# Local attention: q's norm applied on GpSimd, and v projected in the next tile's step

## The chip, the cores and the metric

The kernel runs on one core of one Trainium2 chip. Its time is the device time of one execution in microseconds (us), and a kernel's figure is the median of its runs.

The core has five engines that matter here, each with its own instruction stream that is worked off in order: TensorE (PE in the profile; its weight loads are listed apart as PEld), VectorE (DVE), ScalarE (ACT), GpSimd (POOL) and SyncE (SP), which issues the DMAs. They meet through semaphores. Matmuls read SBUF and write PSUM; GpSimd reads and writes SBUF only.

## The reference

The program is a chain of four blocks over activations of 2048 tokens by 128 features, with a layer norm behind each: an attention, a mixture of experts, a second attention, and a transformer of two layers (`LAYERS = 2`), each with local attention and a gated MLP. The change lies in the local attention alone. Per layer, with 8 heads of 64 and windows of 64 tokens that look back one window:

```python
h = shift_token(x)
q, k, v = jnp.split(h @ wqkv, 3, axis=-1)      # each split into heads
q = l2norm(q) * qs
k = l2norm(k) * ksc
q, k = rotary_xpos(q, k)
o = local_attention(q, k, v)                   # softmax(8 q k^T + mask) v, key windows w-1 and w
x = x + o @ wo
```

`l2norm` divides each head's vector by its own length, one number for each token and head.

## The kernel before

The 2048 tokens are `NT` = 16 tiles of 128; four tiles (`TPB`) are a batch, and t = n % 4 is a tile's place in its batch. Each layer's local attention (`local_attention`) is a loop over the 16 tiles, software pipelined by hand: every engine has a function `step(n)` that works on the scores of tile n, finishes tile n-1 and prepares tiles n+1 and n+2. Tile 0 runs in `first` in layer 0 (it overlaps the end of the second attention), tile 15 in `last`, where the MLP begins. Nothing reorders instructions: an engine does them in the order of the code, and waits where a semaphore's count is not there yet. In the middle of a layer all inputs are in SBUF; DMAs play no part in these steps.

The order of `step(n)` on each engine:

- TensorE: `scores(n, 0)` (first two masks by an identity matmul, L2261, then the products, L2267), `values(n-1, 1)` (L2294, L2304), `project_qk(n+2)` (L2232), the transposes of the probabilities `turn_p(n, 0)` and `turn_p(n, 1)` (L2277), `scores(n, 1)`, `values(n, 0)`, `spread(n-1)` (L2315), `turn_qk(n+1, 0)`, which transposes q, `turn_p(n, 2)`, `turn_qk(n+1, 1)`, which transposes k (both L2251), `turn_p(n, 3)`, `output(n-1)` (L2322), `project_v(n+2)` (L2243). `scores(n+1, 0)` of the next step waits until k of tile n+1 has been copied out of PSUM.
- VectorE: `rowmax` of head pairs 0 and 1 (L2135 and L2140), `squares(n+1)` (sums and their clamp, L2126 and L2130), `copy_pT(n, 0)` (L2144), `rope_sum(n+1)` (L2122), `rowmax` of pairs 2 and 3, `normalise(n-1)` (L2155), `copy_pT(n, 2)`, `reciprocal(n)` (L2149), `rope_c(n+2)` (L2115), `add_y(n-1)` (L2159).
- ScalarE: the exponentials of pairs 0 and 1 (L2039), `copy_o(n-1)` (L2050), `copy_pT(n, 1)` (L2045), `copy_qk(n+2)` (L1997), the exponentials of pairs 2 and 3, `copy_qT(n+1)` (L2019), `copy_pT(n, 3)`, `copy_kT(n+1)` (L2026, L2028), the squares of tile n+2 (L2002), `copy_v(n+2)` (L2012 for three tiles in four, L2015 for all).
- GpSimd: `norms(n+1)` (the powers L1958 and L1967, k's product L1963), `widen(n)` (L1974), `rope_s(n+2)` (two instructions, L1950).

The norm is `rn = ssqc ** -0.5`, a power of 128 x 8 numbers on GpSimd, one instruction for q and one for k. Only k is multiplied by its norm (128 x 512 numbers, into `k_n`). q stays as it comes out of the rotary sum, and its norm enters later as the `scale` of the exponential; so the row maximum needs a second small VectorE instruction, L2140, which multiplies the maximum by `rn`.

`project_v` writes PSUM bank 7 (`m_ps`), which `spread`, `normalise`, `output` and `add_y` also use; it therefore waits for `add_y` of an earlier tile.

Of the kernel before, what the change touches and what calls it, by code (L numbers as in the profile page):

```python
# [15 lines left out]
P = 128  # L16
# [3 lines left out]
TPB = S // P  # L20
# [1795 lines left out]
def local_attention(nc, keep, tiles, layer):  # L1816
# [41 lines left out]
    sqr = sb("sqr", [P, 2 * INNER])  # L1858
    ssq = sb("ssq", [P, 2 * NH2])
    ssqc = sb("ssqc", [P, 2 * NH2])  # L1860
    rn = sb("rn", [P, TPB, 2 * NH2])
    neg_half = sb("neg_half", [P, 2 * NH2])
    qk_c = sb("qk_c", [P, 2, INNER])
    qk_s = sb("qk_s", [P, 2, INNER])
# [2 lines left out]
    qT = sb("qT", [P, 2, PAIRS, P])  # L1867
    kT = sb("kT", [P, 2, 2, 3, P])
    v = sb("v", [P, TPB, INNER])
    negraw = sb("negraw", [P, NH2])  # L1870
    negmax = sb("negmax", [P, NH2])
    den = sb("den", [P, 2, NH2])
    rden = sb("rden", [P, NH2])
# [60 lines left out]
    def gpsimd(pool):  # L1934
# [19 lines left out]

        def norms(n, t):

            pool.wait_ge(ssq_done, n + 1)
            nc.gpsimd.tensor_tensor(rn[:, t, NH2:2 * NH2], ssqc[:, NH2:2 * NH2], neg_half[:, 0:NH2], ALU.pow  # L1958
                                    ).then_inc(rn_step, 1)
            pool.wait_ge(rope_add, n + 1)  # L1960
            pool.wait_ge(rn_step, 2 * n + 1)
            wait_past(pool, qkT_mm, 2 * n)
            nc.gpsimd.tensor_tensor(k_n[:, :].rearrange("p (h d) -> p h d", d=HD2),  # L1963
                                    qk_r[:, 1, :].rearrange("p (h d) -> p h d", d=HD2),
                                    rn[:, t, NH2:2 * NH2, None].broadcast_to([P, NH2, HD2]), ALU.mult
                                    ).then_inc(qk_norm, 1)
            nc.gpsimd.tensor_tensor(rn[:, t, 0:NH2], ssqc[:, 0:NH2], neg_half[:, 0:NH2], ALU.pow  # L1967
                                    ).then_inc(rn_step, 1)
            pool.wait_ge(rn_step, 2 * n + 2)

        def widen(n):
            pool.wait_ge(recip, n + 1)
# [18 lines left out]
    def scalar(act):  # L1991
# [40 lines left out]
        def exps(n, t, k):  # L2032
            j = PAIRS * n + k
            act.wait_ge(max_done, j + 1)
            if k == 0:
                wait_past(act, recip, n - 1)
            for i in range(2):
                u = head(k, i)
                ins = nc.scalar.activation(prob[:, k % 2, keys(t, i)], ps[:, 2 + k % 2, keys(t, i)], ACT.Exp,  # L2039
                                           bias=negmax[:, u:u + 1], scale=rn[:, t, u:u + 1], accum_out=den[:, t % 2, u:u + 1])  # L2040
            ins.then_inc(exp_done, 1)

        def copy_pT(n, t, k):
# [8 lines left out]
        def step(n):  # L2052
            t = n % TPB
            exps(n, t, 0)
            exps(n, t, 1)
            if n:
                copy_o(n - 1)
            copy_pT(n, t, 1)
            if n + 2 < NT:
                copy_qk(n + 2)  # L2060
            exps(n, t, 2)
            exps(n, t, 3)
            if n + 1 < NT:
                copy_qT(n + 1, (t + 1) % TPB)
            copy_pT(n, t, 3)
            if n + 1 < NT:
                copy_kT(n + 1, (t + 1) % TPB)
            if n + 2 < NT:
                squares(n + 2)
            if n + 2 < NT:  # L2070
                copy_v(n + 2, (t + 2) % TPB)

        def last(mlp):

# [12 lines left out]
        def first(low_half):  # L2087

            exps(0, 0, 0)
            exps(0, 0, 1)  # L2090
            copy_pT(0, 0, 1)
            copy_qk(2)
            exps(0, 0, 2)
            exps(0, 0, 3)
            copy_qT(1, 1)
            low_half()
            copy_pT(0, 0, 3)
            copy_kT(1, 1)
            squares(2)
            copy_v(2, 2)  # L2100

        return LocalScalar(step, first, last, copy_qk, squares, copy_v, copy_qT, copy_kT)

    def vector(dve):
# [27 lines left out]
        def rowmax(n, t, k):  # L2132
            dve.wait_ge(s_mm, PAIRS * n + k + 1)
            us = slice(head(k, 0), head(k, 1) + 1, 2)
            nc.vector.tensor_reduce(negraw[:, us],  # L2135
                                    ps[:, 2 + k % 2, 0:2 * KEYS].rearrange("p (i c) -> p i c", i=2) if t
                                    else blocks(t, ps[:, 2 + k % 2, 0:2 * KEYS]), AX.X, ALU.max, negate=True).then_inc(raw_max, 1)
            dve.wait_ge(raw_max, PAIRS * n + k + 1)
            dve.wait_ge(rn_step, 2 * n + 2)
            nc.vector.tensor_tensor(negmax[:, us], negraw[:, us], rn[:, t, us], ALU.mult).then_inc(max_done, 1)  # L2140

        def copy_pT(n, t, k):
            dve.wait_ge(pT_mm, PAIRS * n + k + 1)
# [70 lines left out]
    def tensor(pe, ahead):  # L2214
# [158 lines left out]
        def first(turn_x):  # L2373
# [604 lines left out]
```

## Time and profile before

| | us |
|---|---|
| median of 3 runs | 1655.27 |
| lowest, highest | 1651.87, 1656.19 |
| the profiled execution, its own time | 1658.24 |
| its span in the profile | 1656.5 |
| scores of layer 0's tile 0 start | 1146.23 |
| scores of layer 0's tile 15 start | 1332.01 |
| scores of layer 1's tile 0 start | 1404.25 |
| scores of layer 1's tile 15 start | 1585.65 |

The last four lines are times from the span's start, where the first mask of a tile's scores starts. Over the span TensorE is busy 92%, VectorE 69%, ScalarE 65%, GpSimd 31%. The two stretches of the local attention are some 186 and 181 us of the span for 15 steps each.

A timeline row gives an instruction or a run of like ones: start, duration, engine, line, operation, output from inputs, how many, and in brackets the idle time of its engine before it and what ended it. Matmuls are pipelined, so what a group of them costs TensorE is the distance from its start to the next group's start, not its printed duration.

### The profile page before, as it was taken

The page shows a single profiled execution, that of the slowest core. Times are in us where ns is not written, and L with a number is a line of the kernel's source. Part 1 is how long each engine was busy: PE and PEld are TensorE (multiplying, and loading weights), DVE is VectorE, ACT ScalarE, POOL GpSimd, SP SyncE. Part 2 cuts the span into 40 slices and gives each one's busy share as a digit, 9 for nine tenths or more (in the row PEclk, how much of TensorE's full clock was granted, in tenths as well). Part 3 has the DMA queues.
Part 4 walks back from the last instruction along what each step waited for, and adds up shares of the span by engine and source line. Part 5 has one row for each costly group of instructions (what it writes and reads, how often), then busy time and mean ns, then how long its engine had stood idle before and what let it go on. Part 6 is the DMA issues. An engine that isn't in the chain of part 4 may idle for free. (4 is left out here: it accounts for less than half of the span.)

```text
span 1656.5 us, 30452 instructions
## 1 busy us (share of the span) xinstructions
PE 1525.9 (92%) x10190; PEld 1033.3 (62%) x10190; DVE 1137.0 (69%) x2336; ACT 1083.1 (65%) x2499; POOL 517.0 (31%) x476
## 2 busy tenths in 40 slices
PE   7999999999979999999979999996999888999986
PEld 6777777777667888888854333333566555566654
DVE  2666666666658777777787788864677654767755
ACT  2555555555567888888856577754777755777751
POOL 1222222222232112222110000015767633776732
PEclk9999999999979999999987799978999999999998
DMA  7000000000011221221100000000000000000000
GB/s 236 2 2 0 0 0 0 0 0 0 1 49 57 77 76 64 76 76 55 59 1 1 1 1 1 1 1 1 1 1 1 1 1 0 1 2 1 1 1 26
DMA packets 18993, 36.35 MB, mean 22 GB/s; under 512 B 5764, under 2 KB 11008, under 8 KB 16704
## 3 DMA queue, kind: packets, MB, share of 16 engines
q1 hardware_dynamic: 18896, 35.09, 6.4%
q8 instruction: 57, 0.93, 0.2%
q14 instruction: 40, 0.33, 0.1%
HBM read 33.91 MB, written 1.18 MB: 21 GB/s over the span
## 5 line engine op out<-in xcount | busy, mean ns | idle before, releaser
L915 DVE TENSOR_TENSOR m_hidp<-m_hid,m_hidp 128x512 fp32r<-128x512 f32 x256 | 181.6, 737 | 76.6 <-ACT m_hidp L831 75.4
L305 ACT ACTIVATE a_prob<-ps,a_negmax 128x512 f32<-128x512 f32 (+3 forms) x256 | 134.0, 526 | 146.7 <-DVE a_negmax L381 146.7
L836 ACT ACTIVATE m_hid<-ps,pre_w 128x512 f32<-128x512 f32 x256 | 175.7, 687 | 63.2 <-PE ps L1064 62.5
L1064 PE MATMUL ps<-c_sb_st,m_w1p 128*128 128x512 f32 x768 | 192.1, 399 | 0.0
L1119 PE MATMUL ps<-m_hidp,m_w2p 128*128 128x512 f32 x768 | 190.0, 396 | 0.2 <-DVE m_hidp L915 0.2
L1441 ACT ACTIVATE c_sb_pT<-ps 128x512 f32<-128x512 f32 x256 | 137.4, 601 | 79.6 <-PE ps L1654 78.6
L1511 DVE TENSOR_REDUCE c_sb_negmax<-ps 128x1 f32<-128x512 f32 x240 | 152.7, 684 | 47.2 <-PE ps L1639 47.1
L265 POOL TENSOR_TENSOR a_qk_r<-a_qk_c,a_qk_s 128x512 f32<-128x512 f32 x64 | 81.3, 1270 | 324.0 <-DVE a_qk_s L372 324.0
L2039 ACT ACTIVATE l_sb_prob<-ps,l_sb_negmax,l_sb_rn 128x192 f32<-128x192 f32 (+1 forms) x256 | 124.1, 494 | 69.5 <-DVE l_sb_negmax L2140 69.5
L1064 PEld LDWEIGHTS ps<-c_sb_st,m_w1p 128*128 128x128 f32 x768 | 145.5, 190 | 37.8 <-issue 3.0
L1119 PEld LDWEIGHTS ps<-m_hidp,m_w2p 128*128 128x128 f32 x768 | 144.1, 188 | 35.8 <-DVE m_hidp L915 0.4
L831 ACT ACTIVATE m_hidp<-m_hid 128x512 fp32r<-128x512 f32 x256 | 153.9, 630 | 0.0
L381 DVE TENSOR_REDUCE a_negmax<-ps 128x1 f32<-128x512 f32 (+3 forms) x256 | 112.9, 483 | 23.3 <-PE ps L478 23.3
L2135 DVE TENSOR_REDUCE l_sb_negraw<-ps 128x2 f32<-128x384 f32 (+1 forms) x128 | 66.3, 518 | 76.1 <-PE ps L2267 76.1
L386 DVE COPY a_probT<-ps 128x512 f32<-128x512 f32 (+3 forms) x128 | 61.0, 477 | 81.2 <-PE ps L488 81.2
L500 PEld LDWEIGHTS ps<-a_probT,a_lat 128*64 128x64 f32 x1280 | 68.2, 136 | 66.8 <-issue 61.5
L500 PE MATMUL ps<-a_probT,a_lat 128*64 128x128 f32 x1280 | 98.1, 282 | 10.2 <-issue 9.1
L478 PE MATMUL ps<-a_qkT 64*128 64x256 f32 (+3 forms) x512 | 104.6, 485 | 0.0
L488 PE MATMUL ps<-keep_ident,a_prob 128*128 128x128 f32 x640 | 96.1, 281 | 0.0
L1639 PE MATMUL ps<-c_sb_st 32*128 32x512 f32 x240 | 84.1, 532 | 10.4 <-ACT c_sb_pT L1441 10.4
L1950 POOL TENSOR_TENSOR c_sb_pT<-c_sb_pT,l_sb_tab_s 128x512 f32<-128x512 f32 x64 | 82.7, 1311 | 17.4 <-ACT c_sb_pT L1997 16.8
L759 POOL CAST m_w1p<-pre_w 128x512 fp32r<-128x512 f32 x16 | 10.3, 643 | 245.8 <-DMA pre_w<-w1T 180.6
(247 smaller groups left out, 3253.9 us busy)
## 6 DMA issues: line engine op xcount, KB each, us to landing
m_gate_all<-m_gates_d SPq DMA_DIRECT2D x16, 1024.0 KB, 4.7
pre_w<-w1T SPq DMA_DIRECT2D x14, 258.0 KB, 2.6
pre_w<-w2T SPq DMA_DIRECT2D x14, 256.0 KB, 2.7
pre_wqkv<-wqkv SPq DMA_DIRECT2D x2, 768.0 KB
keep_x<-x SPq DMA_DIRECT2D x1, 1024.0 KB, 10.0
out<-keep_x SPq DMA_DIRECT2D x4, 256.0 KB, 2.5
keep_xT<-xT SPq DMA_DIRECT2D x1, 768.0 KB, 5.2
pre_m_w<-l_w SPq DMA_DIRECT2D x2, 341.0 KB
```

Source lines behind the costliest of these rows:

```text
L305: nc.scalar.activation(prob[:, u % 4, 0:width(p)], score_ps(b, p, j)[:, 0:width(p)], ACT.Exp, bias=negmax[:, u:u + 1], accum_out=den[:, b ...
L381: nc.vector.tensor_reduce(negmax[:, u:u + 1], score_ps(b, p, j)[:, 0:width(p)], AX.X, ALU.max, negate=True).then_inc(max_done, 1)
L478: nc.tensor.matmul(score_ps(b, p, j)[:, 0:width(p)], qkT[r, b % 2, 0, i * P:(i + 1) * P], qkT[r, b % 2, 1, 0:width(p)], start=False, stop= ...
L500: ins = nc.tensor.matmul(o_ps[64 * j:64 * j + 64, i * P:(i + 1) * P], lat[:, b * TPB + t, :], probT[:, j, t * P:(t + 1) * P], start=(t == ...
L831: nc.scalar.activation(hidp[:, c % 2, 0, f, :], hid[:, c % 2, f, :], ACT.Copy).then_inc(high_done, 1)
L836: nc.scalar.activation(hid[:, c % 2, f, :], ps[:, f, :], ACT.Gelu, bias=w1[:, k, FF + f:FF + f + 1]).then_inc(gelu_done, 1)
L915: nc.vector.tensor_tensor(hidp[:, c % 2, 1, f, :], hid[:, c % 2, f, :], hidp[:, c % 2, 0, f, :], ALU.subtract).then_inc(low_done, 1)
L1064: ins = nc.tensor.matmul(ps[:, f, :], w1p[:, k, a, f * P:(f + 1) * P], xp[:, b, c, :], start=(i == 0), stop=(i == 2))
L1119: ins = nc.tensor.matmul(ps[:, 4 + c % 2, :], w2p[:, k, a, f, :], hidp[:, c % 2, b, f, :], start=(f == 0 and i == 0), stop=(f == FB - 1 an ...
L1441: nc.scalar.activation(pT[:, m % 2, g + i, t, :], ps[:, pair(exp_turn(e)).start + i, :], ACT.Exp, scale=SCALE).then_inc(exp_done, 1)
L1511: nc.vector.tensor_reduce(negmax[:, m % 2, t, g + i:g + i + 1], ps[:, pair(max_turn(k)).start + i, :], AX.X, ALU.max, negate=True).then_in ...
L2039: ins = nc.scalar.activation(prob[:, k % 2, keys(t, i)], ps[:, 2 + k % 2, keys(t, i)], ACT.Exp, bias=negmax[:, u:u + 1], scale=rn[:, t, u: ...
```

## The change

Two edits of `local_attention`, together.

First, q is multiplied by its norm on GpSimd, in place, before k. The order in `norms` becomes: power for q, wait for the rotary sum, product for q, power for k, product for k. Before it was: power for k, wait for the rotary sum, product for k, power for q. The transposes of q now wait for q's product. In return the row maximum is final as it comes out of PSUM: L2140, its semaphore and its wait for the norm go, and the exponential has no `scale` from a tile.

Second, v of tile n+1 is projected in step n behind `values(n-1, 1)` and ahead of `project_qk(n+2)`, where v of tile n+2 was projected at the end of step n. ScalarE copies it behind `copy_pT(n, 1)` and ahead of `copy_qk(n+2)`, where it did so at the end of the step. The waits inside `project_v` and `copy_v` are unchanged. No DMA and no SyncE instruction is touched.

```diff
         def norms(n, t):
             pool.wait_ge(ssq_done, n + 1)
-            nc.gpsimd.tensor_tensor(rn[:, t, NH2:2 * NH2], ssqc[:, NH2:2 * NH2], neg_half[:, 0:NH2], ALU.pow
-                                    ).then_inc(rn_step, 1)
-            pool.wait_ge(rope_add, n + 1)
-            pool.wait_ge(rn_step, 2 * n + 1)
-            wait_past(pool, qkT_mm, 2 * n)
-            nc.gpsimd.tensor_tensor(k_n[:, :].rearrange("p (h d) -> p h d", d=HD2),
-                                    qk_r[:, 1, :].rearrange("p (h d) -> p h d", d=HD2),
-                                    rn[:, t, NH2:2 * NH2, None].broadcast_to([P, NH2, HD2]), ALU.mult
-                                    ).then_inc(qk_norm, 1)
-            nc.gpsimd.tensor_tensor(rn[:, t, 0:NH2], ssqc[:, 0:NH2], neg_half[:, 0:NH2], ALU.pow
-                                    ).then_inc(rn_step, 1)
-            pool.wait_ge(rn_step, 2 * n + 2)
+            for w in range(2):
+                nc.gpsimd.tensor_tensor(rn[:, heads(w)], ssqc[:, heads(w)], neg_half[:, 0:NH2], ALU.pow
+                                        ).then_inc(rn_step, 1)
+                if w == 0:
+                    pool.wait_ge(rope_add, n + 1)
+                else:
+                    wait_past(pool, qkT_mm, 2 * n)
+                pool.wait_ge(rn_step, 2 * n + w + 1)
+                nc.gpsimd.tensor_tensor((k_n[:, :] if w else qk_r[:, 0, :]).rearrange("p (h d) -> p h d", d=HD2),
+                                        qk_r[:, w, :].rearrange("p (h d) -> p h d", d=HD2),
+                                        rn[:, heads(w), None].broadcast_to([P, NH2, HD2]), ALU.mult
+                                        ).then_inc(qk_norm, 1)
...
             for i in range(2):
                 u = head(k, i)
                 ins = nc.scalar.activation(prob[:, k % 2, keys(t, i)], ps[:, 2 + k % 2, keys(t, i)], ACT.Exp,
-                                           bias=negmax[:, u:u + 1], scale=rn[:, t, u:u + 1], accum_out=den[:, t % 2, u:u + 1])
+                                           bias=negmax[:, u:u + 1], accum_out=den[:, t % 2, u:u + 1])
...
             copy_pT(n, t, 1)
+            if 1 < n + 1 < NT:
+                copy_v(n + 1, (t + 1) % TPB)
             if n + 2 < NT:
                 copy_qk(n + 2)
...
-            if n + 2 < NT:
-                copy_v(n + 2, (t + 2) % TPB)
...
-            nc.vector.tensor_reduce(negraw[:, us],
+            nc.vector.tensor_reduce(negmax[:, us],
...
-                                    else blocks(t, ps[:, 2 + k % 2, 0:2 * KEYS]), AX.X, ALU.max, negate=True).then_inc(raw_max, 1)
-            dve.wait_ge(raw_max, PAIRS * n + k + 1)
-            dve.wait_ge(rn_step, 2 * n + 2)
-            nc.vector.tensor_tensor(negmax[:, us], negraw[:, us], rn[:, t, us], ALU.mult).then_inc(max_done, 1)
+                                    else blocks(t, ps[:, 2 + k % 2, 0:2 * KEYS]), AX.X, ALU.max, negate=True).then_inc(max_done, 1)
...
             pe.wait_ge(raw_done, min(n + 2, NT))
-            pe.wait_ge(qk_norm if w else rope_add, n + 1)
+            pe.wait_ge(qk_norm, 2 * n + w + 1)
...
                 values(n - 1, (t - 1) % TPB, 1)
+            if 1 < n + 1 < NT:
+                project_v(n + 1, (t + 1) % TPB)
             if n + 2 < NT:
                 project_qk(n + 2, (t + 2) % TPB)
...
                 output(n - 1)
-            if n + 2 < NT:
-                project_v(n + 2, (t + 2) % TPB)
```

`first` loses its `project_v(2, 2)` and `copy_v(2, 2)` in the same way.

## Rows read from the trace of the kernel before

**Rows 1.** Windows of layer 0's steps 4, 5, 6 and 14: busy of PE, PEld, DVE, ACT, POOL; clock; DMA
```profile
1198.90:1210.66 11.76, 10.16 (x80) 6.77 (x78) 8.43 (x17) 9.09 (x26) 8.56 (x7) 1.00 0.01 2
1210.66:1222.71 12.05, 11.44 (x83) 7.40 (x82) 8.66 (x17) 9.73 (x26) 8.68 (x7) 1.00 0.01 1
1222.71:1235.35 12.64, 11.81 (x91) 7.82 (x90) 8.77 (x17) 9.35 (x25) 8.58 (x7) 1.00 0.00 1
1320.91:1332.01 11.10, 9.40 (x85) 6.65 (x84) 7.47 (x16) 7.49 (x23) 7.18 (x6) 1.00 0.01 2
```

**Rows 2.** The chain that ended last, in step 6: start, duration, what
```profile
1229.70 0.65 DVE l_sb_negmax L2140
1230.37 1.10 ACT l_sb_prob L2039 x4
...
1233.98 0.30 DVE keep_x L2159
```

**Rows 3.** Timeline of TensorE in step 6
```profile
1222.71 0.49 PE L2261 MATMUL ps<-pre_wmask,pre_identb 128*128 128x384 bf16 x2
...
1226.97 0.82 PE L2277 MATMUL ps<-keep_ident,l_sb_prob 128*128 128x128 f32 x6
...
1230.07 0.66 PE L2315 MATMUL ps<-keep_ident,c_sb_pT 128*128 128x128 f32 x4
1230.56 0.60 PE L2251 MATMUL ps<-keep_ident,c_sb_pT 128*128 128x128 f32 x4
...
1231.90 0.60 PE L2251 MATMUL ps<-keep_ident,c_sb_pT 128*128 128x128 f32 x4
1232.51 0.55 PE L2277 MATMUL ps<-keep_ident,l_sb_prob 128*128 128x128 f32 x3
...
1234.42 1.10 PE L2243 MATMUL ps<-pre_wqkv,keep_xT 128*128 128x512 f32 x2 [0.48 <-DVE keep_x L2159]
```

**Rows 4.** Timeline of VectorE, ScalarE and GpSimd in step 6, and v's copy
```profile
1227.50 0.56 DVE L2144 COPY c_sb_pT<-ps 128x384 f32<-128x384 f32 x1 [0.67 <-PE ps L2277]
1227.98 1.22 DVE L2122 TENSOR_TENSOR c_sb_pT<-c_sb_pT 128x1024 f32<-128x1024 f32 x1
1228.22 1.02 ACT L1997 ACTIVATE c_sb_pT<-ps 128x1024 f32<-128x1024 f32 x1
1229.27 1.04 POOL L1963 TENSOR_TENSOR c_sb_pT<-c_sb_pT,l_sb_rn 128x512 f32<-128x512 f32 x1 [0.72 <-DVE c_sb_pT L2122]
1230.27 1.64 POOL L1967 TENSOR_TENSOR l_sb_rn<-l_sb_ssqc,l_sb_neg_half 128x8 f32<-128x8 f32 x1
...
1235.96 0.60 ACT L2015 ACTIVATE c_sb_v_all<-ps 128x512 f32<-128x512 f32 x1
```

**Rows 5.** Timeline in layer 0's step 0: power, k's product, and TensorE behind it
```profile
1154.85 1.63 POOL L1958 TENSOR_TENSOR l_sb_rn<-l_sb_ssqc,l_sb_neg_half 128x8 f32<-128x8 f32 x1
...
1156.61 1.04 POOL L1963 TENSOR_TENSOR c_sb_pT<-c_sb_pT,l_sb_rn 128x512 f32<-128x512 f32 x1
...
1157.80 1.08 PE L2251 MATMUL ps<-keep_ident,c_sb_pT 128*128 128x128 f32 x4 [0.90 <-POOL c_sb_pT L1963]
```

**Rows 6.** Timeline of TensorE at the end of layer 0's step 14
```profile
1330.12 0.55 PE L2277 MATMUL ps<-keep_ident,l_sb_prob 128*128 128x128 f32 x3
...
1332.01 0.50 PE L2261 MATMUL ps<-pre_wmask,pre_identb 128*128 128x384 bf16 x2 [0.45 <-ACT c_sb_pT L2028]
```

**Rows 7.** Three lines over the span: durations least/median/most in ns, first and last start
```profile
L2140 DVE TENSOR_TENSOR l_sb_negmax<-l_sb_negraw,l_sb_rn x128: 160/161/999, 1148.4 to 1593.0; 128x2 f32<-128x2 f32 x128
L1974 POOL TENSOR_TENSOR c_sb_pT<-l_sb_rden,l_sb_ones x32: 1041/1857/1939, 1159.3 to 1595.0; 128x512 f32<-128x512 f32 x32
L2115 DVE TENSOR_TENSOR c_sb_pT<-c_sb_pT,l_sb_tab_c x32: 1172/1175/2218, 1123.1 to 1571.9; 128x1024 f32<-128x1024 f32 x32
```

**Rows 8.** Windows in layer 0's step 0, columns as in the first group
```profile
1153.00:1157.00 4.00, 1.50 (x10) 1.05 (x10) 2.41 (x7) 2.02 (x9) 3.52 (x3) 1.00 0.00 0
1158.00:1161.00 3.00, 3.00 (x9) 1.70 (x9) 2.22 (x4) 1.65 (x4) 2.92 (x2) 0.50 0.00 0
```

More of the change, by code:

```diff
@@ L1860, in local_attention @@
     ssqc = sb("ssqc", [P, 2 * NH2])
-    rn = sb("rn", [P, TPB, 2 * NH2])
+    rn = sb("rn", [P, 2 * NH2])
     neg_half = sb("neg_half", [P, 2 * NH2])
@@ L1869, in local_attention @@
     v = sb("v", [P, TPB, INNER])
-    negraw = sb("negraw", [P, NH2])
     negmax = sb("negmax", [P, NH2])
@@ L1900, in local_attention @@
     s_mm = sem("s_mm")
-    raw_max = sem("raw_max")
     max_done = sem("max_done")
@@ L1955, in norms, with heads @@
         def norms(n, t):
+            def heads(w):
+                return slice(w * NH2, (w + 1) * NH2)
             pool.wait_ge(ssq_done, n + 1)
-            nc.gpsimd.tensor_tensor(rn[:, t, NH2:2 * NH2], ssqc[:, NH2:2 * NH2], neg_half[:, 0:NH2], ALU.pow
-                                    ).then_inc(rn_step, 1)
-            pool.wait_ge(rope_add, n + 1)
-            pool.wait_ge(rn_step, 2 * n + 1)
-            wait_past(pool, qkT_mm, 2 * n)
-            nc.gpsimd.tensor_tensor(k_n[:, :].rearrange("p (h d) -> p h d", d=HD2),
-                                    qk_r[:, 1, :].rearrange("p (h d) -> p h d", d=HD2),
-                                    rn[:, t, NH2:2 * NH2, None].broadcast_to([P, NH2, HD2]), ALU.mult
-                                    ).then_inc(qk_norm, 1)
-            nc.gpsimd.tensor_tensor(rn[:, t, 0:NH2], ssqc[:, 0:NH2], neg_half[:, 0:NH2], ALU.pow
-                                    ).then_inc(rn_step, 1)
-            pool.wait_ge(rn_step, 2 * n + 2)
+            for w in range(2):
[10 more added lines that the diff above has]
+                                        ).then_inc(qk_norm, 1)
         def widen(n):
@@ L2099, in first @@
             squares(2)
-            copy_v(2, 2)
         return LocalScalar(step, first, last, copy_qk, squares, copy_v, copy_qT, copy_kT)
@@ L2385, in first @@
             turn_p(0, 0, 3)
-            project_v(2, 2)
         return LocalTensor(step, first, last, project_qk, project_v, turn_qk)
```

## The prediction, made before the changed kernel ran

> **What bounds the kernel now.** I read the windows first, cut where a tile's first mask starts, so that each row is one step. A step of the middle of a layer takes 11.76, 12.05 or 12.64 us, for t = 0, 1 and 2 [rows 1]; t = 3 is like t = 2. TensorE is busy 11.81 of the 12.64. The reader is to see that little idle time is left to win: a perfect version of this order gains some 0.5 to 0.8 us a step, and every wait longer than that is a loss. Step 14, which projects nothing, has 2.4 us less TensorE work than step 6 and is only 1.54 shorter [rows 1]: a second chain, through the other engines, lies close behind the first.
>
> The chain view says which. In step 6 it runs through the rotary sum, the row maximum of pair 2, its product with the norm (0.65), the exponentials, the last transposes, the output product, `add_y` (0.30) and v's projection [rows 2]. So both things that the change removes lie on the chain: L2140, and the stop of TensorE for `add_y`, which is 0.48 of idle time [rows 3].
>
> The timeline of TensorE gives the skeleton of a step, here with the first mask as zero: probabilities' transposes 4.26, q's transposes 7.85, k's transposes 9.19, last transposes 9.80, next mask 12.64 [rows 1, 3]. That of the others shows GpSimd: k's product starts at 6.56 and ends at 7.60 [rows 4], 1.6 us before TensorE asks for it at 9.19. This slack is what the change has to live on.
>
> **The change part by part.** *v's projection* keeps its price. It is 0.93 from its start to the next mask (1234.42 to 1235.35) [rows 1, 3]. At the end of the step that goes, and the 0.48 of waiting with it. It comes back ahead of everything behind `values(n-1, 1)`: the probabilities' transposes start at 4.26 + 0.93 = 5.19. The exponentials of pairs 0 and 1 don't need it and run beside it. `project_v`'s own wait, for an `add_y` of the step before, has been met for long by then; behind it in TensorE's queue stand q and k's projection and the whole second half.
>
> *Its copy on ScalarE* (0.60 [rows 4], and about 0.4 for the low half in three tiles of four) now stands ahead of `copy_qk` and so of the exponentials of pair 2. `copy_qk` started 1.25 behind the probabilities' transposes [rows 3, 4], so now 6.44, with some 0.9 of v 7.4, and with its own 1.02 the exponentials start at 8.4. From there to the last transposes it was 2.14 (1230.37 to 1232.51) [rows 2, 3], so ScalarE would let them start at 10.5.
>
> *L2140 goes*: 0.16 in the median, 0.65 in step 6, up to 1.00 [rows 2, 7], four times a step. Pair 2's maximum would be ready at 7.9, but the exponentials wait for ScalarE until 8.4, so nothing of it shows in the sum in these steps. It counts in the last tile, twice 0.19 (with the gap before it), and in step 1, where it took the 1.00.
>
> *q's product on GpSimd* is the large term, and it isn't q's own. q is ready in time: its transposes are asked for at 7.85 + 0.93 = 8.78, and q's product ends at 8.53. But k's product stood right behind the rotary sum and now stands behind q's product and k's power. In order of time, each duration from a row:
> - probabilities' transposes 5.19; VectorE's copy of them 0.53 later, 5.72 [rows 3, 4];
> - rotary sum 0.48 later, 6.20; first product on GpSimd 1.29 later, 7.49 [rows 4];
> - from that product's start to the power's start 1.00 [rows 4], from a power's start to the product that needs it 1.77 (1.64 of its own and 0.13 of semaphore, 1154.85 to 1156.61 is 1.76) [rows 5]: k's product starts at 10.26 and, 1.04 long, ends at 11.30;
> - TensorE starts k's transposes 0.15 behind the end of the product (1157.65 to 1157.80) [rows 5]: 11.45, where it was 9.19;
> - four transposes take 0.49 from start to start (1230.07 to 1230.56) [rows 3], so the last transposes start at 11.94, 1.4 later than ScalarE's limit of 10.5;
> - from there to the next mask 1.89, where the copy of k ends last (1330.12 to 1332.01) [rows 6]: 13.83.
>
> That is 1.19 more than 12.64. For t = 1 the same sum starts 0.58 earlier in a step that was 0.59 shorter, so it is 1.18 again; for t = 0 and 3 I take the same. The output product runs beside the copies of k, as it did in step 14, where the mask after it waited 0.45 for the copy of k [rows 6], so TensorE's own work doesn't set the end.
>
> Bounds of what no row shows. How long q's product takes: it has k's shape and form, in place instead of into `k_n`. I take k's 1.04, the nearest row [rows 4]; the ends are 1.00, its least distance to the next start, and the 1.86 of a product of that shape that VectorE holds up [rows 7]. That is 0 to +0.8 a step, or up to 1709 for the run.
>
> The sum for the run. Steps 2 to 13 of two layers: 24 x 1.19 = 28.6. Step 1, where the 1.00 stall goes: +0.4 each, 0.8. Step 14: the probabilities' transposes wait there for the exponentials, not for TensorE, so v's 0.93 falls into that wait and GpSimd's 2.77 less k's slack is left: the mask at 12.0 for 11.10 [rows 1], 0.9 each, 1.8. Step 0: in layer 0 TensorE already waited 0.90 for k's product [rows 5], so nearly all of the 2.77 comes through, less 0.3 to 0.5 in which v's projection held the end: +2.3; in layer 1 the product had 1.4 to spare: +1.4. Last tile: -0.4 each, -0.8. Start of layer 1: 0 to 1.0, as a rotary product of VectorE starts within 0.1 us of where k's product would: 0.3. Sum 34.4. It is made against the profiled execution, 1658.2, which stands 3.0 above the median of the runs; I carry the difference to the median: 1655.3 + 34.4 = 1689.7.
>
> **The rivals.** *Faster: k comes in time.* If k's product started by 8.9 instead of 10.26, the exponentials would set the end: 10.5 + 1.89 = 12.4 in three tiles of four and 12.0 where v has no low half, 0.2 and 0.7 less than now, some 0.35 x 24 = 8 with about 1 from the last tiles: 1646. This needs 1.4 us off a chain of which every link has a row; k's power, 1.63 and 1.64 in the rows [rows 4, 5], would have to run beside q's product. Against it: GpSimd works in order in every row. 6%.
>
> *The pair of VectorE and GpSimd.* In the trace the two engines block each other: L2140 took 0.65 where k's product ran beside it and ended with it, and `widen` takes 1.04 alone in the least case but 1.86 in the median, where `rope_c` of VectorE (L2115, 1.18) overlaps it [rows 2, 7]. In the changed kernel `rope_c` follows the exponentials: I get about 10.5 to 10.6 for its start and 10.26 for k's product. In that order `rope_c` waits and nobody misses it. If it comes first, k's product waits for up to its 1.2 us: 24 steps of it are +29, 1719; if only in the tiles without a low half, where the two are closest, +7, 1697. 12% for the large case.
> The Trainium skill, page "SBUF — State Buffer", section "🔬 SBUF: two separate sides", says the same as a rule: the shared ports are an exclusive lock, and whichever of the two starts first has it for the whole instruction, also against a VectorE operation with two SBUF inputs. By that rule the trace agrees (L2140's 0.65), and the rule speaks against this change, which puts 1.04 more of such GpSimd work into each step; what it costs hangs on the order of the two starts, as above.
>
> *The clock falls.* TensorE will stand idle for some 1.7 us ahead of k's transposes and 0.5 ahead of the masks. In layer 0's step 0, four microseconds at 1.50 busy were followed by a granted clock of 0.50, that is 1.2 GHz, for 3 us [rows 8]; in the steps now it is 1.00, 2.4 GHz. If that came in each step, some 1.5 us more of TensorE work each, +36 on top: 1726. Over the stretch from 9.8 to 13.8 I count 1.9 busy, more than in that row. 8%.
>
> *The loss is smaller, or nothing.* Some link overlaps more than I take, and the step grows by 0.3 to 0.8: 1662 to 1678, 8%; or gain and loss cancel to within 5 us, 3%.
>
> **How the numbers follow.** The forecast with its own errors, 1679 to 1702: 63%. Blocked pair or clock: 20%. Smaller loss 8%, no change 3%, faster 6%. The range from 1672 to 1710 takes in the forecast, half of the smaller loss, and the part of the blocked pair that hits some tiles only; it leaves out about 2 in 10. About 0.3%, 5 us, is what a measurement of this kernel can tell from no change; by it, faster 0.06, same 0.04, slower 0.90.
>
> **What would show it.** In the changed profile: steps near 13.0, 13.2 and 13.8 us. k's product about 2.8 behind the end of the rotary sum. TensorE's k transposes with some 1.7 us of idle time before them that GpSimd ended, and the next mask released by the copy of k. The stop for `add_y` and L2140 gone. `rope_c` stretched where k's product is under way. The prediction is wrong if TensorE doesn't wait at k's transposes, if k's product starts before 9, or if the granted clock of the steps isn't 1.00.

## The result, and the profile after

The changed kernel takes 1715.8 us in the median (1712.5 to 1718.4, four runs) against 1653.6 for the kernel before on the same chip: a ratio of 1.037, with a 95% interval of 1.0349 to 1.0391. The prediction was slower, 1689.7, with a range up to 1710. The direction was right; the loss is 62 us where 34 were forecast, and lies above the range.

The windows, cut where a tile's first mask starts, answer to [rows 1]. Columns: stretch, length, busy time of PE, PEld, DVE, ACT, POOL, granted clock, DMA.

```profile
1202.52:1217.21 14.69, 11.42 (x78) 8.15 (x79) 6.59 (x12) 8.51 (x27) 11.30 (x9) 0.85 0.01 1
1217.21:1231.41 14.20, 12.18 (x84) 7.97 (x82) 8.68 (x14) 8.64 (x27) 8.06 (x7) 0.92 0.01 2
1231.41:1247.03 15.62, 12.78 (x91) 9.31 (x92) 7.40 (x12) 8.54 (x26) 11.68 (x9) 0.89 0.01 2
1247.03:1260.71 13.68, 11.66 (x92) 7.80 (x90) 8.69 (x14) 8.82 (x27) 7.91 (x7) 1.00 0.00 0
...
1347.63:1359.61 11.98, 9.84 (x87) 7.06 (x87) 6.60 (x12) 7.54 (x24) 8.30 (x7) 1.00 0.00 0
```

These are t = 0, 1, 2, 3 and step 14. Before, t = 2 and 3 were alike at 12.64; now they are 15.62 and 13.68, and of the four only t = 3 runs at a clock of 1.00. So there are two losses: one that every step has, and one that t = 3 escapes.

The profiled span is 1716.0 against 1656.5, 59.5 more. Steps 2 to 13 take 174.6 and 174.8 us in the two layers for 147.3 each: +54.8. Steps 0 and 1 add 7.8 and step 14 of both layers 1.8. The rest, -4.9, lies outside these steps: the local attention starts 2.8 earlier, the stretch between the layers is 0.9 shorter and the tail 1.2.

The timeline of step 6 (t = 2; first mask 1231.41) tells where the loss sits. Columns: start, duration, engine, line, what, and in brackets the idle time before it with what ended it.

```profile
1231.41 0.50 PE L2259 MATMUL ps<-pre_wmask,pre_identb 128*128 128x384 bf16 x2 [0.45 <-ACT c_sb_pT L2030]
...
1236.54 0.82 PE L2275 MATMUL ps<-keep_ident,l_sb_prob 128*128 128x128 f32 x6
1237.54 1.22 DVE L2123 TENSOR_TENSOR c_sb_pT<-c_sb_pT 128x1024 f32<-128x1024 f32 x1
1238.84 1.04 POOL L1968 TENSOR_TENSOR c_sb_pT<-c_sb_pT,l_sb_rn 128x512 f32<-128x512 f32 x1 [1.98 <-DVE c_sb_pT L2123]
1239.84 1.64 POOL L1961 TENSOR_TENSOR l_sb_rn<-l_sb_ssqc,l_sb_neg_half 128x8 f32<-128x8 f32 x1
...
1241.09 0.56 DVE L2142 COPY c_sb_pT<-ps 128x384 f32<-128x384 f32 x1
1241.57 0.19 DVE L2147 RECIPROCAL l_sb_rden<-l_sb_den 128x8 f32<-128x8 f32 x1
1241.62 2.13 POOL L1968 TENSOR_TENSOR c_sb_pT<-c_sb_pT,l_sb_rn 128x512 f32<-128x512 f32 x1
1241.68 1.17 DVE L2116 TENSOR_TENSOR c_sb_pT<-c_sb_pT,l_sb_tab_c 128x1024 f32<-128x1024 f32 x1
1243.89 1.09 PE L2249 MATMUL ps<-keep_ident,c_sb_pT 128*128 128x128 f32 x4 [2.84 <-POOL c_sb_pT L1968]
```

Counted from the mask: probabilities' transposes 5.13, rotary sum 6.13, q's product 7.43, k's power 8.43, k's product 10.21. The prediction had 5.19, 6.20, 7.49, 8.49, 10.26. Up to there the chain is as forecast. Then k's product (L1968, from 1241.62) takes 2.13 where it took 1.04 [rows 4], and `rope_c` (L2116), 0.06 later, takes its full 1.17. The order was as forecast, but its effect was the opposite: the one that the trace lists first is held up.

In t = 3 the same two start 0.24 apart, and there it is `rope_c` that is held up:

```profile
1257.22 1.04 POOL L1968 TENSOR_TENSOR c_sb_pT<-c_sb_pT,l_sb_rn 128x512 f32<-128x512 f32 x1
1257.46 1.88 DVE L2116 TENSOR_TENSOR c_sb_pT<-c_sb_pT,l_sb_tab_c 128x1024 f32<-128x1024 f32 x1
1258.41 0.63 PE L2249 MATMUL ps<-keep_ident,c_sb_pT 128*128 128x128 f32 x4 [1.57 <-POOL c_sb_pT L1968]
```

t = 1 is like t = 3 (1227.92 and 1228.16). In t = 0 `rope_c` is ahead, by 0.19, and k's product takes 1.88:

```profile
1211.98 1.17 DVE L2116 TENSOR_TENSOR c_sb_pT<-c_sb_pT,l_sb_tab_c 128x1024 f32<-128x1024 f32 x1
1212.17 1.88 POOL L1968 TENSOR_TENSOR c_sb_pT<-c_sb_pT,l_sb_rn 128x512 f32<-128x512 f32 x1
1214.20 1.09 PE L2249 MATMUL ps<-keep_ident,c_sb_pT 128*128 128x128 f32 x4 [2.71 <-POOL c_sb_pT L1968]
```

Over the span (durations least/median/most in ns, first and last start; q's products are in the row too):

```profile
L1968 POOL TENSOR_TENSOR c_sb_pT<-c_sb_pT,l_sb_rn x64: 1041/1042/2134, 1137.3 to 1642.8; 128x512 f32<-128x512 f32 x64
```

The Trainium skill, page "SBUF — State Buffer", section "🔬 SBUF: two separate sides", has the pair as an exclusive lock that goes to the one that starts first. In t = 0, 1 and 3 the trace agrees; in t = 2 it doesn't, and the measurement decides: a start 0.06 ahead by the trace was not enough. Whether the pair is granted later than the start that the trace shows, or the trace's starts of the two engines are a little off against each other, no run tells. A start 0.13 ahead was enough, at the start of layer 1:

```profile
1427.83 1.04 POOL L1968 TENSOR_TENSOR c_sb_pT<-c_sb_pT,l_sb_rn 128x512 f32<-128x512 f32 x1
1427.96 1.99 DVE L2116 TENSOR_TENSOR c_sb_pT<-c_sb_pT,l_sb_tab_c 128x1024 f32<-128x1024 f32 x1
```

One rival is close by. In t = 2 VectorE's reciprocal (L2147) starts 0.05 ahead of k's product, in t = 3 0.14 behind it, so it could be the reciprocal that holds the product. `e3_rope_c_waits` below has the reciprocal at the same place without `rope_c` behind it, and there the product takes 1.04.

The other part of what t = 0, 1 and 2 lose is the clock. Windows of TensorE's idle stretch in step 6 and of what follows, columns as above:

```profile
1241.00:1244.00 3.00, 0.16 (x2) 0.14 (x2) 1.78 (x4) 0.47 (x1) 2.86 (x3) 0.92 0.01 3
1244.00:1247.00 3.00, 3.00 (x15) 3.00 (x16) 0.00 (x0) 1.34 (x4) 3.00 (x3) 0.51 0.03 8
```

After 2.84 us of idle time the granted clock is 0.51, that is 1.2 GHz, for the 3 us that follow. After the 1.57 of t = 3 it stays at 1.00. The low level that follows the 2.71 of t = 0 reaches past the next mask, so that t = 1, whose own idle time is 1.57 too, pays for it:

```profile
1217.20:1218.20 1.00, 1.00 (x6) 0.36 (x5) 0.29 (x1) 0.64 (x1) 0.31 (x1) 0.50 0.00 0
```

### The profile page after: what moved, and what is told of

Same layout as the page of the kernel before. It is cut to its first block and busy times, and to the rows that moved or that the text cites. A ratio compares the mean times of both kernels' runs of the same rounds, so it can differ in the third digit from the quotient of the medians.

```text
span 1716.0 us, 30256 instructions
## 1 busy us (share of the span) xinstructions
PE 1540.1 (90%) x10190; PEld 1054.6 (61%) x10190; DVE 1111.0 (65%) x2208; ACT 1056.8 (62%) x2499; POOL 553.2 (32%) x508
## 5 line engine op out<-in xcount | busy, mean ns | idle before, releaser
L1961 POOL TENSOR_TENSOR l_sb_rn<-l_sb_ssqc,l_sb_neg_half 128x8 f32<-128x8 f32 x64 | 104.7, 1636 | 81.1 <-DVE l_sb_ssqc L2131 81.1
L2041 ACT ACTIVATE l_sb_prob<-ps,l_sb_negmax 128x192 f32<-128x192 f32 (+1 forms) x256 | 101.0, 411 | 48.1 <-DVE l_sb_negmax L2136 48.1
L2249 PE MATMUL ps<-keep_ident,c_sb_pT 128*128 128x128 f32 x256 | 45.8, 309 | 70.8 <-POOL c_sb_pT L1968 70.8
L2047 ACT ACTIVATE c_sb_pT<-ps 128x384 f32<-128x384 f32 (+1 forms) x64 | 29.8, 465 | 129.2 <-PE ps L2275 128.6
L1968 POOL TENSOR_TENSOR c_sb_pT<-c_sb_pT,l_sb_rn 128x512 f32<-128x512 f32 x64 | 79.0, 1235 | 65.1 <-DVE c_sb_pT L2123 60.5
```

Source lines behind the costliest of these rows:

```text
L1961: nc.gpsimd.tensor_tensor(rn[:, heads(w)], ssqc[:, heads(w)], neg_half[:, 0:NH2], ALU.pow).then_inc(rn_step, 1)
L1968: nc.gpsimd.tensor_tensor((k_n[:, :] if w else qk_r[:, 0, :]).rearrange("p (h d) -> p h d", d=HD2), qk_r[:, w, :].rearrange("p (h d) -> p ...
```

## The experiments

The theory after the comparison: three parts add up. The chain through GpSimd makes k late (as forecast); the pair of VectorE and GpSimd holds k's product in t = 0 and 2; the longer idle time of those steps brings the clock down. Rivals: the pair matters only through the exponentials, which set `rope_c`'s start; or the clock falls by itself. The kernels ran in three sets, each with the kernel before beside it (medians 1656.5, 1655.9 and 1653.1), so across sets the ratios are compared; their intervals are some 0.2 to 0.45% wide to each side, 3 to 7 us. The middle of a layer, steps 2 to 13, is what the experiments are read by, since the start of the local attention moves by up to 10 us (1138 to 1148) from one profile to another, which isn't traced to the edits. Such a sum comes from one profile of each kernel, but like steps in it mostly agree within 0.02 us where the clock is 1.00.

### The two halves apart

`e1_q_alone` is the changed kernel with v's projection and copy back at the end of the step:

```diff
-            if 1 < n + 1 < NT:
-                project_v(n + 1, (t + 1) % TPB)
...
+            if n + 2 < NT:
+                project_v(n + 2, (t + 2) % TPB)
```

> Only q's half of the change: q multiplied on GpSimd ahead of k, v's projection left at the end of the step. Theory (k's product comes too late): k's product starts 2.77 us later than before and TensorE waits for it; a step with t = 2 is 10.5 for k's transposes + 0.49 + 0.38 to the output product + 1.53 to v's projection + 0.93 = 13.8 for 12.64, and k's product (9.3) starts ahead of rope_c (9.5), so nothing blocks it: about +34, 1688. Rival (the two halves simply add up, and q's half is all of the loss): 1716. Rival (v's projection in the middle is what hurts): within 10 us of before, 1655 to 1665.

Measured: 1754.5, ratio 1.0587 (1.0546 to 1.0627), above all three. Steps 1 to 13 take 14.9 to 17.1 us, and steps 2 to 13 of a layer 191 together. Timeline of a step with t = 1 (mask 1220.04):

```profile
1228.80 2.14 POOL L1968 TENSOR_TENSOR c_sb_pT<-c_sb_pT,l_sb_rn 128x512 f32<-128x512 f32 x1
1228.86 1.18 DVE L2117 TENSOR_TENSOR c_sb_pT<-c_sb_pT,l_sb_tab_c 128x1024 f32<-128x1024 f32 x1
1231.08 0.63 PE L2250 MATMUL ps<-keep_ident,c_sb_pT 128*128 128x128 f32 x4 [2.84 <-POOL c_sb_pT L1968]
...
1234.19 1.68 PE L2242 MATMUL ps<-pre_wqkv,keep_xT 128*128 128x512 f32 x2 [0.48 <-DVE keep_x L2158]
1235.70 0.49 PE L2260 MATMUL ps<-pre_wmask,pre_identb 128*128 128x384 bf16 x2
```

Two things are to be seen. The pair is blocked here in t = 1 too, and so it is in every step of the middle (k's product takes 1.82 to 2.14), where the expectation had it free. And behind k's late transposes stand the output product, the stop for `add_y` and v's projection, 4.62 from k's transposes to the next mask at a mean clock of 0.63, where step 6 of the changed kernel has 3.14 at 0.52. So v's move is worth far more once k is late than in the kernel before (2.1% between the ratios of `e1_q_alone` and the change): it takes work from behind the late link. How the 2.1% divide between that and the pair, which is blocked in more steps here, isn't shown.

`e2_v_alone` is the kernel before with v's move only.

> Only v's half: v of the next tile projected behind the scores, norms as before. Theory: k's product is in time (starts 7.5, asked for at 10.1), and ScalarE's exponentials set the end of a step at 10.5 + 1.9 = 12.4 for 12.64 in three tiles of four: 0.2 to 0.7 gained a step, 1642 to 1650. Rival (v's move costs the step its 0.93, since everything behind it is later): 1675 to 1680.

Measured: 1648.8 (ten runs), ratio 0.9962 (0.9939 to 0.9985). Steps of t = 1 and 2:

```profile
1204.05:1216.19 12.14, 11.37 (x83) 7.39 (x83) 9.57 (x17) 9.62 (x27) 8.79 (x7) 1.00 0.00 1
1216.19:1228.74 12.55, 11.75 (x90) 7.82 (x90) 9.46 (x17) 9.23 (x26) 8.58 (x7) 1.00 0.01 2
```

Before, they took 12.05 and 12.64 [rows 1]. Steps 2 to 13 take 146.3 for 147.3: 0.1 to 0.2 gained in three steps of four, where 0.2 to 0.7 were expected. Step 14 is longer, 11.8 for 11.1. So inside the local attention the profile shows a net gain of only 0.8 us, for some 6 by the ratio; the rest lies in its earlier start (1139.3 for 1146.2), which isn't traced to the change. That the time lies in the expected band is in the main luck. v's move alone is worth little.

### The pair of VectorE and GpSimd

`e3_rope_c_waits` makes `rope_c` wait until k's product is done, which puts VectorE in second place in every tile:

```diff
+                dve.wait_ge(qk_norm, 2 * (n + 2))
                 rope_c(n + 2, (t + 2) % TPB)
```

> The changed kernel with one wait more: rope_c on VectorE waits until k's product is done, so the two never ask for the shared pair at once with rope_c in front. Theory (in tiles t = 2 and t = 0 rope_c came first, k's product took 2.1 and 1.9 instead of 1.04, and the longer idle time of TensorE then dropped its clock): k's product takes 1.04 everywhere, the granted clock of the steps is 1.00, steps of 13.1, 13.2, 13.8 and 13.7: 1688 to 1694. Rival (the clock falls from the 1.6 us that TensorE waits anyway): the steps behind keep a clock under 1.00, 1705 or more. Rival (rope_c's delay is itself on the chain): no gain, 1716 or more.

Measured: 1694.3, ratio 1.0213 (1.0173 to 1.0253). Step t = 2:

```profile
1237.53 1.04 POOL L1968 TENSOR_TENSOR c_sb_pT<-c_sb_pT,l_sb_rn 128x512 f32<-128x512 f32 x1
1238.61 2.05 DVE L2116 TENSOR_TENSOR c_sb_pT<-c_sb_pT,l_sb_tab_c 128x1024 f32<-128x1024 f32 x1 [0.94 <-POOL c_sb_pT L1968]
1238.72 0.63 PE L2250 MATMUL ps<-keep_ident,c_sb_pT 128*128 128x128 f32 x4 [1.75 <-POOL c_sb_pT L1968]
```

k's product is 1.04 again, though the reciprocal stands where it stood:

```profile
1237.48 0.19 DVE L2147 RECIPROCAL l_sb_rden<-l_sb_den 128x8 f32<-128x8 f32 x1
```

So it is `rope_c` that held the product, not the reciprocal. (`rope_c` itself now takes 2.05, with `widen` of GpSimd ahead of it from 1238.53; nothing waits for that.) TensorE waits 1.75, and most steps are 12.93, 13.12, 13.70 and 13.70 for t = 0 to 3. Steps 2 to 13 take 162.6 a layer for 174.7: one more wait, which delays an engine, wins 24 us.

Not all of the clock's loss is gone. In t = 0 TensorE waits 1.87 or 1.88 for k's product, and in three of the six such steps of the middle the clock falls after it, here for 3 us (t = 0, k's transposes to the next mask); those steps and the ones behind them lose 4.5 us in all:

```profile
1265.56:1268.57 3.01, 3.01 (x14) 2.95 (x15) 1.94 (x1) 1.46 (x4) 3.01 (x2) 0.50 0.00 0
```

`e4_dead_scale` gives the exponentials a scale of one from a tile again, so that they last as long as before and push `rope_c` back:

```diff
-                                           bias=negmax[:, u:u + 1], accum_out=den[:, t % 2, u:u + 1])
+                                           bias=negmax[:, u:u + 1], scale=ones[:, 0:1], accum_out=den[:, t % 2, u:u + 1])
```

> The changed kernel, but each exponential takes its scale from a tile of ones, which changes no value. The exponentials of the changed kernel take 0.42 us, those of before with a scale from a tile 0.51. Theory (the order of two starts decides): four slower exponentials put rope_c 0.36 later, behind the start of k's product in t = 2 (was 0.06 behind it... now 0.3 after) and in t = 0 (0.19), so k's product takes 1.04 and the clock stays: 1690 to 1700, faster by 15 or more with more work. Rival (the work of ScalarE counts): the same as the change or up to 10 slower, 1716 to 1726.

Measured: 1714.3, ratio 1.0337 (1.0299 to 1.0376), no different from the changed kernel, where 1690 to 1700 was expected: the theory fell, and it fell in two ways. In t = 2 nothing moved:

```profile
1243.51 2.13 POOL L1968 TENSOR_TENSOR c_sb_pT<-c_sb_pT,l_sb_rn 128x512 f32<-128x512 f32 x1
1243.57 1.17 DVE L2116 TENSOR_TENSOR c_sb_pT<-c_sb_pT,l_sb_tab_c 128x1024 f32<-128x1024 f32 x1
```

So in t = 2 it isn't the exponentials that set `rope_c`'s start. In step 6 above it is the copy of the probabilities (L2142, from 1241.09), behind which it stands with a reciprocal, and that copy goes by TensorE's order. In t = 0 the edit did what it was meant to do, and it didn't help: `rope_c`, 0.19 ahead in the changed kernel, now starts 0.03 behind, and k's product still takes 2.12.

```profile
1213.59 2.12 POOL L1968 TENSOR_TENSOR c_sb_pT<-c_sb_pT,l_sb_rn 128x512 f32<-128x512 f32 x1
1213.62 1.18 DVE L2116 TENSOR_TENSOR c_sb_pT<-c_sb_pT,l_sb_tab_c 128x1024 f32<-128x1024 f32 x1
```

So the exponentials do set `rope_c`'s start in t = 0, but a lead of 0.03 by the trace is as useless to k's product as one of 0.06.

### The clock

`e5_filler` is the changed kernel with 16 needless transposes of the identity in front of k's transposes, into the buffer that these fill next:

```diff
+                for r in range(4):
+                    for a in range(4):
+                        nc.tensor.transpose(ps[:, 1, a * P:(a + 1) * P], ident[:, :], ident[:, :])
                 turn_qk(n + 1, 1)
```

> The changed kernel with 16 needless transposes of the identity (into k's PSUM bank, which is free there) between the transposes of pair 2's probabilities and those of k: they fill TensorE's idle time, about 2 us, and change no wait. Theory (the second half of what I had missed is the clock): k's product is still held up in t = 2 and t = 0 (2.1 and 1.9 us), but the granted clock of the steps stays 1.00, so t = 2 takes 14.9 for 15.6, t = 0 13.9 for 14.7, t = 1 13.3 for 14.2: 1699 to 1704, with more work on TensorE. Rival (the low clock lay beside waiting and cost nothing): 1716 or more.

Measured: 1696.5, ratio 1.025 (1.0222 to 1.0278), 2.5 under the expected band. Steps t = 0, 1, 2, and k's product in the last of them:

```profile
1200.26:1214.02 13.76, 11.89 (x95) 8.48 (x95) 6.88 (x13) 8.25 (x27) 10.38 (x9) 1.00 0.00 1
1214.02:1227.14 13.12, 12.67 (x99) 9.15 (x99) 8.40 (x13) 8.89 (x27) 8.99 (x8) 1.00 0.00 1
1227.14:1241.93 14.79, 13.24 (x107) 9.58 (x107) 7.68 (x13) 8.48 (x26) 10.84 (x9) 1.00 0.01 2
...
1237.35 2.13 POOL L1968 TENSOR_TENSOR c_sb_pT<-c_sb_pT,l_sb_rn 128x512 f32<-128x512 f32 x1
```

The pair is as blocked as before, and the clock is 1.00. More work on TensorE made the kernel some 1.2% faster by the ratios, and 17 us by the steps.

`e10_wait_and_filler` has the edits of both, and leaves the late chain alone.

> The changed kernel with rope_c waiting for k's product and with the 16 needless transposes: neither the blocked pair nor the clock is left, only k's late product. Theory (three terms that add up over the steps 2 to 13 of a layer: late product +13.1, blocked pair +5.7, clock +8.5): those steps take 160.4 us in both layers (steps of 12.9, 13.1, 13.7, 13.7), granted clock 1.00: 1683 to 1690. Rival (blocked pair and clock are the same loss counted twice, removing either is enough): no faster than the better of the two single runs, 1694 or more.

Measured: 1689.8, ratio 1.0212 (1.0168 to 1.0257). The steps are 12.93, 13.12, 13.70 and 13.70. The first masks of t = 2 and 3:

```profile
1227.56 0.50 PE L2260 MATMUL ps<-pre_wmask,pre_identb 128*128 128x384 bf16 x2 [0.46 <-ACT c_sb_pT L2030]
1241.26 0.50 PE L2260 MATMUL ps<-pre_wmask,pre_identb 128*128 128x384 bf16 x2 [0.45 <-ACT c_sb_pT L2030]
```

By the ratios this run can't be told from `e3_rope_c_waits` (1.0213), and its interval overlaps that of `e5_filler`; it is the sums of the steps that separate them, and they come out at the 160.4 expected. With these three the loss of steps 2 to 13 comes apart (sum of a layer; both layers together):

| kernel | steps 2 to 13 | what is in it | cost, both layers |
| --- | --- | --- | --- |
| before | 147.3 | | |
| both edits (`e10_wait_and_filler`) | 160.3 | the late chain | +26.1 |
| filler alone (`e5_filler`) | 166.1 | and the blocked pair | +11.5 |
| changed | 174.6, 174.8 | and the clock | +17.2 |

The last two shares hang on the order in which they are taken away: with the blocked pair gone first (`e3_rope_c_waits`) the steps win 24.2, and only 4.5 are left for the clock. The clock costs 17.2 because the blocked pair makes the idle time long.

### The late chain itself

Both powers need only the sums of squares, not the rotary sum. `e6_powers_first` issues them ahead of it:

```diff
-                if w == 0:
-                    pool.wait_ge(rope_add, n + 1)
-                else:
+            pool.wait_ge(rope_add, n + 1)
+            pool.wait_ge(rn_step, 2 * n + 2)
+            for w in range(2):
+                if w:
                     wait_past(pool, qkT_mm, 2 * n)
-                pool.wait_ge(rn_step, 2 * n + w + 1)
```

> The changed kernel with both powers ahead of the wait for the rotary sum, so that only q's product stands between the sum and k's product. Theory (the power, 1.77 from start to product, is what makes k late; a product alone fits): k's product starts at 8.5 and ends at 9.5 in the step, TensorE does not wait for it, L2140 and the stop for add_y are gone and pay: steps of about 12.1 for t = 2 and 3, 11.5 for t = 1 and t = 0, 1638 to 1645. Rival (a second product on GpSimd is too much in itself, through the shared pair or its length): over 1665.

Measured: 1641.2, ratio 0.9924 (0.9899 to 0.9949): faster than both kernels, and in the expected band. Step t = 2:

```profile
1218.91 3.24 POOL L1961 TENSOR_TENSOR l_sb_rn<-l_sb_ssqc,l_sb_neg_half 128x8 f32<-128x8 f32 x2 [1.02 <-DVE l_sb_ssqc L2131]
1221.23 1.22 DVE L2123 TENSOR_TENSOR c_sb_pT<-c_sb_pT 128x1024 f32<-128x1024 f32 x1
1222.52 2.04 POOL L1968 TENSOR_TENSOR c_sb_pT<-c_sb_pT,l_sb_rn 128x512 f32<-128x512 f32 x2 [0.38 <-DVE c_sb_pT L2123]
1224.71 0.63 PE L2249 MATMUL ps<-keep_ident,c_sb_pT 128*128 128x128 f32 x4
```

In the middle of a layer TensorE no longer waits for k, and the steps are 11.15, 11.68, 11.92 and 11.98. GpSimd does the same work; only the order differs.

`e9_one_power` makes one power of 16 columns of the two:

```diff
+            nc.gpsimd.tensor_tensor(rn[:, :], ssqc[:, :], neg_half[:, :], ALU.pow).then_inc(rn_step, 2)
+            pool.wait_ge(rope_add, n + 1)
+            pool.wait_ge(rn_step, 2 * n + 2)
```

> Both halves of the change, with the one power of 128 x 16 ahead of the wait. Both theories: the power is off the path as the two powers were in the run with both halves and the powers first (1641), since the rotary sum comes later there: steps of 11.9 as in that run, 1637 to 1645. If the single power took more than 3.6 it would hold q's product up, and the run would be slower than 1645.

Measured: 1639.4, ratio 0.9921 (0.9893 to 0.995). The steps of t = 0 and 1 take 11.15 and 11.42; t = 2:

```profile
1220.63:1232.55 11.92, 11.47 (x90) 7.83 (x91) 7.68 (x13) 8.48 (x26) 9.41 (x7) 1.00 0.02 3
```

The two can't be told apart by their times; by the steps 2 to 13 this one is 0.8 a layer shorter (139.4 for 140.2). Is this q's half or v's? `e7_powers_first_q_alone` has v at its old place:

> As the run before, but with v's projection left at the end of the step: q's half alone, with both powers ahead. Theory: k's product ends at 8.6, just ahead of where TensorE asks for it, and the row maxima without L2140 start the exponentials of pair 2 0.6 earlier: a step of t = 2 of 12.1 for 12.64, 1638 to 1645. Rival (with v's projection not in front, k's product and rope_c meet again, or the product is late by its own 1.04): 1655 or more.

Measured: 1695.0, ratio 1.0238 (1.0214 to 1.0262), not the 1638 to 1645 expected. The timeline shows a new hold-up:

```profile
1209.17 4.19 POOL L1961 TENSOR_TENSOR l_sb_rn<-l_sb_ssqc,l_sb_neg_half 128x8 f32<-128x8 f32 x2 [1.38 <-DVE l_sb_ssqc L2132]
1210.66 1.22 DVE L2124 TENSOR_TENSOR c_sb_pT<-c_sb_pT 128x1024 f32<-128x1024 f32 x1
1214.69 0.63 PE L2250 MATMUL ps<-keep_ident,c_sb_pT 128*128 128x128 f32 x4 [2.16 <-POOL c_sb_pT L1968]
```

The two powers take 4.19 instead of 3.24: the second starts at 1210.77, 0.11 behind the rotary sum, takes 2.59 for 1.64, and so is held for about as long as the sum still runs. In t = 1 it starts 0.72 behind the sum and takes 1.98. With v's projection moved, the rotary sum comes later, and both powers are under way before it (1221.23 above).

`e8_one_power_q_alone` removes just that: one power, issued ahead of the sum, v at its old place.

> q's half alone (v's projection at the end of the step), with q's and k's powers as one instruction of 128 x 16 ahead of the wait for the rotary sum. In the run with two powers there, the second one started behind the start of the rotary sum and took 2.57 for 1.64. Theory (an instruction of GpSimd that starts while a two-input one of VectorE runs is held up until that ends; one that has started is not, and does not hold the other up for its whole length): the single power takes about 2.9 (1.01 for 4 columns, 1.64 for 8), starts ahead of the rotary sum, is not stretched, and the rotary sum keeps its 1.22; q's product starts at about 7.0 for 7.9, a step of t = 2 about 12.5 for 13.6: 1648 to 1662. Rival (the lock is held for the whole of a power): the rotary sum is stretched to 2 or more, and the step stays at 13.5: 1690 or more.

Measured: 1657.6 (ten runs) against 1653.1, ratio 1.0028 (1.0009 to 1.0046), in the expected band.

```profile
1198.65 2.90 POOL L1960 TENSOR_TENSOR l_sb_rn<-l_sb_ssqc,l_sb_neg_half 128x16 f32<-128x16 f32 x1 [1.43 <-DVE l_sb_ssqc L2130]
1200.07 1.22 DVE L2122 TENSOR_TENSOR c_sb_pT<-c_sb_pT 128x1024 f32<-128x1024 f32 x1
```

The power is under way when the sum starts; neither is stretched. Steps 2 to 13 take 146.3, 1.0 less than before; steps 0 and 1 together are longer (32.5 us in layer 0 and 24.1 in layer 1, for 27.4 and 23.0), and step 14 is 11.4 for 11.1. Against the ratio of 1.0587 of `e1_q_alone` that is 5.6%, and all of it is in what GpSimd does ahead of the sum: 3.4% with the two powers issued first (`e7_powers_first_q_alone`), 2.1% more with one wide power in their place.

## Why the prediction was right and wrong

*The late chain: right.* This was the term that carried the sum. Forecast 1.19 a step, measured with the other two causes removed 1.06 (t = 2 and 3), 1.17 (t = 0) and 1.07 (t = 1). With the steps at the ends `e10_wait_and_filler` has 26.1 + 7.4 + 1.8 = 35.3 for the forecast's 34.4, which also counts -0.5 outside these steps. That its time, 1689.8, is the forecast's 1689.7 is chance: the kernel before was at 1653.1 beside it, while the forecast starts from 1655.3. k's product starts at 10.21 for 10.26; TensorE's idle time before k's transposes is 1.57 to 1.88 in `e3_rope_c_waits` for "some 1.7". From k's transposes to the next mask it was 2.30 in t = 3, for 2.38 in the sum.

*How long k's product takes: where it failed.* The chain has k's product "1.04 long", and the blocked pair stands in the sum at nothing. It took 2.13 in t = 2 and 1.88 in t = 0: 11.5 us of the run, and 17.2 more through the clock. The ground for the nothing was that `rope_c` starts at 10.5 to 10.6 and k's product at 10.26, and "In that order `rope_c` waits and nobody misses it". Three things were wrong in it:
- `rope_c`'s start was taken from the exponentials. In t = 2 it follows the copy of the probabilities and the reciprocal, at 10.27; `e4_dead_scale` shows that the exponentials have no say there. The 8.4 from which the prediction counts has the copy of v's low half in it, and t = 2 is the step without one: there the exponentials of pair 2 start at 7.85. I had left VectorE's own queue out.
- That it is enough to be first. 0.06 ahead, k's product is held for 1.09; 0.13 and 0.24 ahead it isn't. `e3_rope_c_waits` shows that it is `rope_c` which holds it.
- "For t = 0 and 3 I take the same". t = 0 was never worked out. There k's product starts at 9.65 and `rope_c` at 9.46: outright second. It needed one more line of the same sum.

The bound that I gave the product (up to 0.8 a step, 1709 for the run) was for q's product. q's took 1.04; k's, which I had not bounded, took 2.13.

*The rival of the blocked pair: right in kind.* Its small case was 7 us for the tiles without a low half, the large case 29 for all. The tiles without a low half are those of t = 2, and by `e5_filler` and `e10_wait_and_filler` they cost 6 x 1.09 = 6.5. t = 0, which nothing was worked out for, added 6 x 0.83 = 5.0, and together it is 11.5.

*The clock: priced as a rival of its own.* The prediction gave it 8%, since the idle time of some 1.7 leaves more work around it than the row of step 0 had, and `e3_rope_c_waits` bears that out for most steps (162.6 a layer, 2.3 above `e10_wait_and_filler`). Not for all: in t = 0 the wait is 1.88, and there the clock fell in half of the steps. And with the pair blocked the idle time is 2.71 to 2.84, which I had not asked about. The two rivals aren't independent: the first brings on the second, 11.5 and 17.2 together. This is why the range was too narrow. It took in each of them for a part and never both.

*Small terms.* L2140 and the stop for `add_y` are gone, as forecast. Step 14: 0.9 a layer, right. Steps 0 and 1, forecast +2.3 and +1.4 for step 0 and 0.8 for step 1 of both layers, 4.5 in all, came to +7.8: step 0 grew by 2.0 and 3.8, step 1 by 0.3 and 1.7. In layer 1 that is 3.8 more than forecast: the pair is blocked in its step 0 too (k's product takes 1.82), the clock falls after a wait of 2.71, and step 1 is longer with it; `e10_wait_and_filler` has 12.48 and 13.12 there for 13.93 and 14.64. The last tiles, forecast at -0.4 each, lie in the stretch between the layers, 0.9 shorter, and in the tail, 1.2 shorter.

*The rival "k comes in time": it was there to be had.* I gave it 6% because each link had a row, and for the code as changed the low chance was right. `e6_powers_first` makes the rival true by issuing one link, k's power, ahead of the wait, and gets 1641.2 for the 1646 that this rival was given. The prediction saw only that the power "would have to run beside q's product".

## What to carry to other kernels

When an operation moves onto an in-order queue, ask which instruction then stands between the late input and the product that needs it; what doesn't need the late input goes in front of the wait. Here that alone turned +3.7% into -0.8%. Where two engines block each other, work out both starts in every kind of step, take leads of less than 0.1 us in the trace as undecided, and carry the longer idle time on to the clock before giving the rivals their chances.

## What the runs showed of the hardware

- A product of 128x512 on GpSimd beside a 128x1024 operation of VectorE: 0.24 us ahead it keeps its 1.04 and VectorE takes 1.88, 0.13 ahead likewise (VectorE 1.99); 0.06 ahead it takes 2.13 and VectorE keeps 1.17, 0.03 ahead likewise (2.12, `e4_dead_scale`). Where between 0.06 and 0.13 it turns, no run shows.
- A power on GpSimd that is under way doesn't hold the rotary sum (1.22 beside a power of 2.90), nor the sum the power. One that starts 0.11 behind the sum takes 2.59 for 1.64 (`e7_powers_first_q_alone`). Why one that runs doesn't hold the sum, no run shows.
- A power of 8 columns takes 1.64, one of 16 takes 2.90: one wide one is 0.38 shorter than two.
- The exponential without a scale from a tile is shorter: 421 ns in the median, for 506 before and 507 in `e4_dead_scale`, which have it.

```profile
L2041 ACT ACTIVATE l_sb_prob<-ps,l_sb_negmax x256: 357/421/448, 1146.1 to 1653.6; 128x192 f32<-128x192 f32 x96, 128x128 f32<-128x128 f32 x32
```

- In the changed kernel's steps TensorE's granted clock stayed at 1.00 behind each idle stretch of 1.57 us and was 0.50 to 0.53 for 3 us behind each of 2.71 and 2.84. In `e3_rope_c_waits` it stayed at 1.00 behind 1.75 and fell in three of six steps behind 1.87 or 1.88. The length of one idle stretch doesn't settle it: in `e1_q_alone` four stretches of 2.84 in twenty were followed by a clock of 1.00.
